# A second bank of probabilities turned through DRAM at the end, and LayerNorms on ScalarE at the beginning

## The reference

```
h = jnp.maximum(_layernorm(x, axis=-1), 0.0)
q = _split_heads(h @ Wq + bq); k = _split_heads(h @ Wk + bk); v = _split_heads(h @ Wv + bv)
scores = jnp.einsum('bhqd,bhkd->bhqk', q, k) / sqrt(HD)
scores = scores + beta * adj_e
scores = jnp.where(adj_e > 0, scores, -9e15)
probs = jax.nn.softmax(scores, axis=-1)
out = jnp.einsum('bhqk,bhkd->bhqd', probs, v)
x = x + out.transpose(0, 2, 1, 3).reshape(...)
```

## Time and profile before

| | |
|---|---|
| median of 3 runs | 509.98 us |
| the profiled execution | 510.33 us |
| its span in the trace | 508.5 us |
| PE busy | 494.7 us, 97% |
| ACT busy | 452.4 us, 89% |
| DVE busy | 434.9 us, 86% |
| POOL busy | 174.9 us, 34% |
| granted TensorE clock | 1.00 in nearly every stretch |

### The profile page before, as it was taken

How to read it: one execution, slowest core, us unless ns; L and a number is a source line. 1 busy time by engine, 2 the same in 40 slices (tenths; PEclk the granted TensorE clock), 3 DMA queues, 4 the chain that set the end, 5 groups by cost and what they waited for, 6 DMA issues and landing times.

```text
span 508.5 us, 17222 instructions
## 1 busy us (share of the span) xinstructions
PE 494.7 (97%) x5130; PEld 412.9 (81%) x5130; DVE 434.9 (86%) x2254; ACT 452.4 (89%) x1831; POOL 174.9 (34%) x262
## 2 busy tenths in 40 slices
PE   8989999999999999999999999999999999999995
PEld 7767888888888888888888888888888888888774
DVE  5898988988898898998899889889889987876796
ACT  3649999999999999999989999998999999899795
POOL 5521044334324423433432432343343333322311
PEclk9999999999999999999999999999999999999999
DMA  8565677777777778777777877777787676445311
GB/s 245 186 182 174 202 240 249 220 224 242 258 223 251 238 220 241 234 256 230 242 227 226 246 234 246 242 235 234 216 261 227 214 222 202 147 128 170 119 60 48
DMA packets 113388, 107.59 MB, mean 212 GB/s; under 512 B 12608, under 2 KB 98496, under 8 KB 113344
## 3 DMA queue, kind: packets, MB, share of 16 engines
q1 hardware_dynamic: 113344, 107.14, 67.3%
HBM read 56.63 MB, written 50.46 MB: 211 GB/s over the span
## 4 chain that ended last, share of the span: by engine, by line
PE 87%; ACT 4%; DVE 1%; issue 1%; DVEq 0%
PE G_ps L938 38%; PE S_ps L1003 18%; PE PT_ps L987 10%; PE S_ps L955 10%; PE PT_ps L971 10%; ACT probs L581 3%; ACT probsT L604 1%; PE G_ps L987 1%; DVE probsT L800 0%; ACT probs_blocks L596 0%; ACT qk L612 0%; ACT h_hi L626 0%; PE S_ps L1028 0%; DVE w_raw L826 0%; PE PT_ps L993 0%
## 5 line engine op out<-in xcount | busy, mean ns | idle before, releaser
L774 DVE CUSTOM_DVE_ANT_0 probs<-S_ps,bias 128x128 f32<-128x128 f32 x768 | 167.5, 287 | 54.2 <-PE S_ps L955 54.2
L581 ACT ACTIVATE probs<-probs,negmax 128x128 f32<-128x128 f32 x532 | 206.0, 396 | 0.0
L938 PE MATMUL G_ps<-h_hi,w_hi 128*128 128x512 f32 x288 | 116.9, 406 | 2.1 <-DVE h_lo L720 1.1
L938 PE MATMUL G_ps<-h_hi,w_lo 128*128 128x512 f32 x288 | 117.8, 409 | 0.0
L938 PE MATMUL G_ps<-h_lo,w_hi 128*128 128x512 f32 x288 | 116.4, 404 | 0.0
L596 ACT ACTIVATE probs_blocks<-probs,negmax 128x128 f32<-128x128 f32 x236 | 92.1, 391 | 25.1 <-DVE negmax L774 24.5
L581 ACT ACTIVATION_READ_ACCUMULATOR probs<-probs,negmax 128x1 f32 x532 | 103.7, 195 | 0.0
L503 POOL TENSOR_TENSOR var_eps<-meanvar,eps_col 128x1 f32<-128x1 f32 x64 | 13.2, 207 | 243.7 <-DVE meanvar L697 243.6
L527 POOL TENSOR_TENSOR w_raw<-w_raw,rinv 128x384 f32<-128x384 f32 x58 | 57.4, 989 | 51.0 <-issue 50.7
L552 POOL TENSOR_TENSOR w_raw<-w_raw,x_ring 128x384 f32<-128x384 f32 x63 | 64.7, 1028 | 25.5 <-DVE w_raw L787 17.4
L938 PEld LDWEIGHTS G_ps<-h_hi,w_hi 128*128 128x128 f32 x288 | 54.1, 188 | 18.5 <-ACT qk L612 3.8
(11 more groups left out here) (64 smaller groups left out, 749.1 us busy)
## 6 DMA issues: line engine op xcount, KB each, us to landing
probs_rows<-probs_blocks SPq DMA_DIRECT2D x59, 256.0 KB, 2.0
probs_moved<-probs_rows SPq DMA_DIRECT2D x236, 64.0 KB, 2.5
out_dram<-w_raw SPq DMA_DIRECT2D x63, 192.0 KB, 2.1
x_ring<-in_x_dram SPq DMA_DIRECT2D x61, 192.0 KB, 2.8
w_raw<-out_rows SPq DMA_DIRECT2D x116, 96.0 KB, 2.4
xhat_rows<-xhat_blocks SPq DMA_DIRECT2D x28, 384.0 KB, 3.6
xhat_moved<-xhat_rows SPq DMA_DIRECT2D x112, 96.0 KB, 2.5
out_rows<-xhat SPq DMA_DIRECT2D x15, 384.0 KB, 2.3
```

The costliest lines, as they stand in the source:

```text
L581: last = nc.scalar.activation(p, p, ACT.Exp, bias=negmax[:, e, j * KC + m:j * KC + m + 1], scale=TURN, accum_out=rowsum[:, e, m * HC + j:m ...
L774: last = nc.vector.tensor_tensor_reduce(probs[:, a, j, m, :], S_ps[:, j, m * N:(m + 1) * N], bias[(z.par + 1) % 2][:, z.s, :], 1.0, LARGES ...
L938: mm = nc.tensor.matmul(G_ps[:, u % 2, :], pairs[n][0], pairs[n][1], start=(n == 0), stop=(n == len(pairs) - 1))
```

## The change

There are three parts.

1. Sequences 52 to 59 (`FIRST_R2 = B - 3 * GROUP`, so `a` in groups 14 and 15's slots) send bank 1 through DRAM as well. Its exponentials follow those of bank 0 in `exponentials_ahead(z, 1)` (flag `Q2`), go to a part of `x_ring` that is no longer used, and SyncE writes and reads them with `late_rows` (`read_late`, flag `R2`). VectorE does a second block transpose, `transpose_probs(z, 1)`. TensorE's four transposes of bank 1 and ScalarE's copy of it go.
2. Sequence 59's exponentials of banks 0 and 1 are done ahead in slot (15,3), and both banks come through DRAM in slot (16,0). TensorE transposes bank 2 alone there, and ScalarE copies it.
3. The LayerNorms of sequences 4 to 11 are done by ScalarE (`normalise`, an activation with scale `rstd` and bias `shift`); GpSimd computes `shift = -mean * rstd` for each. VectorE keeps those of 12 and 13, now in slot (1,1), where it also turns the blocks of two sequences (`self.parts`), which it did before in (1,0) and (1,1).

For this, groups 14 and 15 of TensorE are outside its loop (`PE_LOOP` from `(2, NG - 1)` to `(2, NG - 3)`).

```
-    ACT_LOOP, PE_LOOP = (2, NG - 3), (2, NG - 1)
+    ACT_LOOP, PE_LOOP = (2, NG - 3), (2, NG - 3)
+    FIRST_R2 = B - 3 * GROUP
...
+        late_blocks = x_ring[:, 0:HC * FOUR]
+        late_moved = x_ring[:, HC * FOUR:3 * HC * FOUR].rearrange("p (i n) -> p i n", i=2)
...
-                self.R = self.E and not self.F
-                self.Q = self.A and self.P and not (n == NG - 1 and s == GROUP - 1)
+                self.first_f = first_f = n == NG and s == 0
+                self.R = self.E and (first_f or not self.F)
+                self.Q = self.A and self.P
+                self.Q2 = self.static and self.Q and 4 * (n - 1) + s >= FIRST_R2
+                self.R2 = self.static and self.R and 4 * (n - 1) + s - 1 >= FIRST_R2
...
                     elif n == 0:
-                        self.norms = ([4], [6], [7], [8, 9])[s]
+                        self.norms = []
+                        self.act_norms = ([4], [5], [], [])[s], ([], [6], [7], [])[s], ([], [], [], [8, 9])[s]
...
                     elif n == 1 and s == 0:
-                        self.norms, self.late_norms, self.stats, self.masks = [10, 11], [12], [12, 13], [3]
+                        self.norms, self.stats, self.masks = [], [12, 13], [3]
+                        self.act_norms = [10, 11], [], []
                     elif n == 1 and s == 1:
-                        self.masks = [4, 5]
+                        self.norms, self.stats, self.masks = [12, 13], [14], [4, 5]
...
+            def read_late(z):
+                sp.wait_ge(late_rows_written, 16 * (z.e - FIRST_R2 + 1))
+                for c in range(HC):
+                    came = late_rows[(z.s - 1) % 2, :, c * FOUR:(c + 1) * FOUR].rearrange("(r p) n -> p r n", r=HC)
+                    goes = late_moved[c * HD:(c + 1) * HD, (z.s - 1) % 2, :].rearrange("p (r n) -> p r n", r=HC)
+                    sp.dma_start(goes, came).then_inc(late_blocks_moved[(z.s - 1) % 2], 16)
...
+                if z.R2:
+                    read_late(z)
...
+                if z.Q2:
+                    sp.wait_ge(probs_ready[1], z.a + 1)
+                    sp.dma_start(late_rows[z.s % 2, :, :], late_blocks).then_inc(late_rows_written, 16)
...
+                if by_scalar(q):
+                    pool.wait_ge(rstd_ready, q + 1)
+                    nc.gpsimd.tensor_scalar(shift[:, s:s + 1], meanvar[:, s, 0:1], rstd[:, s:s + 1], -1.0, ALU.mult, ALU.mult).then_inc(shift_ready, 1)
...
+            def normalise(z, q):
+                s, at = z.place(q)
+                act.wait_ge(shift_ready, q - GROUP + 1)
...
+                nc.scalar.activation(goes, came, ACT.Identity, bias=shift[:, s:s + 1], scale=rstd[:, s:s + 1]).then_inc(xhat_by_scalar, 1)
...
+                if z.Q2:
+                    exponentials_ahead(z, 1)
...
                 if z.R:
-                    transpose_probs(z)
+                    transpose_probs(z, 0)
+                if z.R2:
+                    transpose_probs(z, 1)
...
-                pe.wait_ge(pT_stored[0], z.o + 1)
+                pe.wait_ge(pT_stored[1 if z.static and FIRST_R2 <= z.o < B - GROUP else 0], z.o + 1)
...
-                if z.E:
+                if z.E and not z.R2:
                     transpose_probs(z, 1)
```

179 lines of the change are left out of this document (107 added, 72 removed).

## The result

| | before | changed |
|---|---|---|
| time, median | 510.32 us (509.92 to 512.31, 4 runs) | 517.67 us (515.40 to 518.28, 4 runs) |
| profiled execution: time, span | 510.33, 508.5 us | 517.95, 516.1 us |
| mean granted clock of TensorE | 0.999 | 0.989 |

The changed kernel is slower: 1.0128 times the time before (95% interval 1.0106 to 1.0151). The forecast was 505.0 us.

The account below looks back on a forecast made before the run. TensorE, busy 494.7 of 508.5 us, was taken as the bound; 2.4 (start) + 1.55 (bank 1) + 1.0 (sequence 59) = 4.95 us off 510.33 gave 505.4, or 505.0 at the median; range 503.6 to 507.6.

Parts of the forecast that it names:

- Part 1: Groups 14 and 15: bank 1 through DRAM saves 0.39 us in each of seven slots, 1.55 us after losses.
- its line on the DMAs: SyncE's added write and four reads per slot fit its over 2 us to spare; landings 1.8 to 2.7 us after issue.
- rival B: Groups 14 and 15: the ScalarE and VectorE chain binds, 0.3 to 0.4 us more per slot; 506.6 us, chance 0.12.
- Rival C: Late reads make TensorE's product wait for VectorE's second transpose; slower when a read takes some 4.6 us; chance 0.05.
- the 3.8: Second trip's reads: a `late_moved` landing beyond 3.8 us would show the prediction wrong; each of eight slots loses the excess.
- Part 3: Start: LayerNorms moved from VectorE to ScalarE remove TensorE's early waits, 2.4 us saved, between 1.0 and 2.8.
- the waits of 1.08 and 1.02: Start: TensorE's waits for `h_lo` of group 1 (1.08 us) and the store of q unit 0 (1.02 us) go.
- The 0.40: Start: TensorE's 0.40 us wait ahead of 42.49 for a ScalarE copy goes as well, or comes back in part.
- Part 2: Sequence 59, slot (16,0): VectorE begins the next maxima at +6.64 instead of +7.68; 1.04 us saved, between 0.3 and 1.4.
- Rival A: Start gains nothing, as ScalarE or VectorE follow closely and waits return some slots later; 507.4 us, chance 0.11.
- D: All TensorE waits in (16,0) and the closing slots vanish and the start gives 2.8 us; 503.8 us, chance 0.06.

Follow-up runs that it names:

- e2: Changed kernel without the second DRAM trip (bank 1 transposed by TensorE) and with TensorE's loop as before: 508.98 us median, tail 99.6 us.
- e13: Changed kernel with the output's transfers in groups 14 and 15 issued by GpSimd instead of SyncE, all bytes moved: 513.82 us median, tail 104.1 us.
- e9: Changed kernel with the second trip carrying a quarter of its bytes, same count of issues, output not the reference's: 513.66 us median, tail 105.0 us.
- e10: Changed kernel with a quarter of the second trip's bytes, read by one DMA instead of four, output not the reference's: 509.06 us median, tail 99.5 us.
- e1: Kernel before with only TensorE's loop ended two groups earlier, so groups 14 and 15 are written out: 510.12 us median, tail 100.6 us.
- e4: Changed kernel with TensorE's loop up to group 15, second trip in full, bank 1's transposes made for nothing: 511.96 us median, tail 102.4 us.
- e3: Kernel before with ScalarE's LayerNorms at the start alone: 508.60 us median, tail 100.2 us.
- e14: Changed kernel with GpSimd issuing the output's transfers in groups 14 and 15 and TensorE's loop as before: 510.95 us median, tail 101.2 us.
- e15: Kernel before with ScalarE's LayerNorms at the start and slot (1,2)'s projection matmuls ahead of its first product: 509.33 us median, tail 100.2 us.
- e8: Changed kernel with the second trip from sequence 56 on instead of 52: 511.84 us median, tail 101.8 us.
- e5: Changed kernel with the second trip's write and reads issued by GpSimd instead of SyncE, TensorE's code written out: 516.82 us median, tail 104.8 us.

## Why the prediction was wrong

**Part 1 is the step that failed**, in its line on the DMAs: "a write (0.34 us) and four reads (1.75 us) more a slot, in 7.0 us of which it has over 2 to spare". Forecast: 1.55 us saved. Measured: 10.2 us lost (the tails of the changed kernel and of e2). Four things were wrong with it.

- It took the idle time of SyncE as free. That time was where SyncE stood ready for ScalarE's data, so a longer order moves every issue back. I had the write at 7.0 us after its sequence's scores, the last read issued at 10.7 and landed at 12.5 to 13.4. Sequence 53 (scores 420.92) had its write at 8.0, the last read at 15.1 and the landing at 17.4 (438.34), and the product wanted it at 15.7. e13 shows this term with all bytes moved (5.8 us), e9 and e10 the issues (5.5) and the bytes (4.8). These aren't shares of one sum: once SyncE has idle time again, taking off more brings nothing.
- It didn't count TensorE's instructions. The end of TensorE's loop is among the edits, and the prediction gives it no cost. It brings five packets that come with issues of SyncE 0.8 to 2.1 us too long: 0.3 us by themselves (e1), and on top of the second trip up to 7.5 us (109.9 against 102.4 in e4, in spite of the transposes saved), of which the longer slots of e4 have a share that wasn't measured.
- It let every landing be at most 2.7 us. Beside a full order and the packets some took 4.2 to 4.9 us, and one of these is behind the second wait.
- It had no price for what can follow a long wait: the clock at 0.50 to 0.71 for several microseconds, behind two of the three.

Right in part 1: the saving of four transposes (0.39 forecast; an undisturbed slot was 0.45 us shorter), ScalarE's copy as a short wait (0.23 us at 422.10, in (14,1) rather than (15,0)), and that the loop over ScalarE and VectorE doesn't bind (rival B): no wait of TensorE in the three slots was for it.

**Rival C** had the mechanism's end, the product waiting for the second transpose, and the wrong way to it. It asked for a read of 4.6 us from issue to landing. The late transfers landed after 2.1 us in the median and 4.2 at most, and the reads of the first trip after 2.2 and 3.3, where before had 2.0 and 2.7:

```profile
DMA to landing us min/median/max: 1.9/2.1/4.2
```

```profile
DMA to landing us min/median/max: 1.9/2.2/3.3
```

The one of 4.2 us is beyond the 3.8 that the prediction named as a sign of being wrong, and is rival C's own way, in one slot, (15,2). In (14,3) and (15,3) the reads were issued late rather than slow. Its chance of 0.05 rested on landings alone.

**Part 3, 2.4 us saved.** It was 1.98 in the changed kernel's profile, and e3's median is 1.3 us under before's, with an interval that includes no change: the waits of 1.08 and 1.02 are gone, scores of sequence 3 began at 47.45 (46.8 forecast). The 0.40 did not go but grew to 1.73: VectorE's transpose of sequence 0 came at 39.87, a little beyond the 39.3 to 39.7 that I gave, but it ends 0.7 us after that, and TensorE was ready at 38.95. I had set its start against the time at which TensorE wants its end. ScalarE's LayerNorm took 0.70 us, not 0.60:

```profile
L685 ACT ACTIVATE xhat_blocks<-x_ring,shift,rstd x4: 695/697/698, 25.8 to 27.6; 128x384 f32<-128x384 f32 x4
```

That is outside my bounds of 513 and 682 ns; the Trainium skill's figures ("ScalarE: Activation LUTs", What ACT_TABLE_LOAD costs) gave 692, and the trace agrees.

**Part 2, 1.0 us saved.** The scores of sequences 60 to 63 in e2, with a wait in (16,1) between them:

```profile
472.83 0.95 PE L1040 MATMUL S_ps<-qk 32*128 32x128 f32 x24
...
478.09 0.95 PE L1040 MATMUL S_ps<-qk 32*128 32x128 f32 x24
...
483.95 0.66 PE L1071 MATMUL G_ps<-ident,probs 128*128 128x128 f32 x4 [0.58 <-ACT probs L632]
...
484.54 0.95 PE L1040 MATMUL S_ps<-qk 32*128 32x128 f32 x24
...
489.80 0.95 PE L1040 MATMUL S_ps<-qk 32*128 32x128 f32 x24
```

(16,0) took 5.26 us instead of e3's 6.49, (16,1) 6.45 instead of 5.26, (16,2) 5.26 instead of 5.88, together 0.66. The gain of (16,0) came, and larger than forecast. That "from (16,1) on VectorE sets the pace" with an unchanged length was wrong: in (16,1) the chain runs through ScalarE's exponentials from 478.68 to 483.91, and most of the gain was given back there.

**Rival A**, that the start gains nothing, was wrong as a rule and right in some executions: of 13 profiles with the new start and the old place of the product, six were at 405.97 to 406.23 us at sequence 51, two at 406.9, five at 408.1 to 410.0 (before: 408.21).

The terms that were measured give 510.33 - 2.0 - 0.6 + 10.2 = 517.9 us, as the profiled execution has it (517.95). This is bookkeeping and no test, since the 10.2 is itself a difference of two tails and holds all that isn't named.

The prediction's own sums hold, but for its range: it starts from "D's 503.6" where D is 503.8. Nothing rests on it.

## What to carry to other kernels

Before transfers are added to an engine's order, add up what that order issues per step and ask what its idle time waits for: idle time ahead of a wait for data is the reserve that keeps later transfers on time, and here 24 of 48 us busy was comfortable and 42 of 48 was not. At 34 of 48 it depended on the rest: no loss with a quarter of the added bytes (e10), 3.8 us with all of them (e13). Allow for transfers that land late as well as for issues that go out late. An edit that writes out a loop brings instruction traffic; it cost 0.3 us here while the engine that issues DMAs had slack, so test it alone and with the rest. Where TensorE comes to wait for 2 us or so, look at the granted clock behind it: it fell behind two waits of three in the changed kernel.

## What the runs showed of the hardware

- A 16 KB packet of TensorE's instructions goes with one DMA issue of SyncE that takes 0.5 to 2.1 us longer than its 0.43 us (five of five in the changed kernel, four of five in e1; in groups 14 and 15 of e2 and e4, without such packets, no issue is that long).
- In the changed kernel transfers issued at 460 us, beside such a packet, landed after 4.2 to 4.9 us, where before none of these trips took over 3.4. A packet isn't shown to be the reason: e14, which has none there, has a transfer of 4.7 us.
- The product at 439.18 behind a wait of 2.57 us ran at a reduced clock (1.08 us instead of 0.86). In the start, a single wait of 1.2 to 1.84 us never brought the clock down in the eight profiles that have one, and one of 2.15 to 2.94 us did in all five; but in e15 two waits of 1.43 and 1.23 us within 3 us did. In the tail a wait of 2.69 us (changed kernel, 464.85) and one of 2.65 us (e8, 474.64) left it at 1.00, and one of 2.57 us did not. So the length of a wait alone doesn't tell.
- The same four reads, issued by GpSimd instead of SyncE, took 0.55 us each instead of 0.43, and landed 0.7 to 0.8 us later in the median (2.8 us in e5).
- That the packets cause the long issues rather than only come with them is shown by e1, which changed nothing else. Through which part of the DMA system they do it was not tried.
